# Local attention of a gated transformer: the last 128 queries' scores in other PSUM banks, ahead of the transposed probabilities of the 128 before them

## Chip, cores and metric

One core of one Trainium2 chip runs the whole kernel. The metric is the device time of one execution in microseconds (us). The kernel before was run three times.

## What is computed

The kernel is four blocks in a row on a stream x of 2048 tokens of width 256: cross-attention with 16 heads, a feed-forward block, a second cross-attention, and a small local transformer of two layers. Only the last one is touched. One of its layers, cut from the reference:

```python
h = shift_token(x)                       # the second half of the width moves one token on
q, k, v = split(h @ wqkv)                # 8 heads of 64
q, k = rotary_xpos(l2norm(q) * qs, l2norm(k) * ksc)
# windows of 128 queries; each looks at its own 128 keys and the 128 in front
sim = where(mask, -max, einsum('bhwid,bhwjd->bhwij', 8 * bq, bk))
o = einsum('bhwij,bhwjd->bhwid', softmax(sim), bv)
x = x + o @ wo
h = shift_token(x)
h = (h - mean(h)) / sqrt(var(h) + 1e-5) * lg + lb
a, g = split(h @ w1 + b1)
x = x + (a * gelu(g)) @ w2 + b2
```

## The kernel before

`windowed_attention` does the attention half of a layer, `shifted_ffn` the other half. Each is one block of the program: its instructions start only when all engines have ended the block in front. Every engine has an order written out by hand: a Python loop `for w in range(ST + 1)` with ST = 16 windows of 128 queries, in which each engine calls small functions for window w and its neighbours. Semaphores tie the engines together; `after(engine, name, n)` waits until n steps of that name are done. `base` is the count of windows in earlier layers. LAST or window 15 is the last, window 14 the one in front of it.

For one window, in the order of the data:

- TensorE `turn` transposes the rotated queries and keys (8 transposes, `d_rotated`) into PSUM banks 3 and 4. ScalarE `move` copies them to `qT` and `kT` (two copies). `qT` has one buffer.
- TensorE `score` makes the scores of 8 heads in two groups of 4 (g = 0, 1), into banks 3, 4 and 5, 6. VectorE `mask` adds the mask and `maxima` takes the row maxima, per group. ScalarE `expo` makes the exponentials of a group, with their sums.
- TensorE `turn_probs` transposes the probabilities of a group (8 transposes of `d_probs`), again into banks 3, 4 and 5, 6. ScalarE `move_probs` copies them to `d_probsT`.
- VectorE `invert` takes the inverse sums, GpSimd `expand` spreads them over the width, TensorE `spread` transposes them into bank 7, ScalarE `move_spread` copies them to `d_spread_in`.
- TensorE `apply` multiplies probabilities and values into bank 2 (`V_BANK`), VectorE `normalize` scales the result into `d_heads_outT`, TensorE `mix` multiplies by wo, again into bank 2, and VectorE `add` adds that to the stream `d_Z`.

While a window is in work, the projections of window w + 3 (split fp16 matmuls, lines 77 to 79) and the rotation of w + 2 run too. In the last windows there are none left. There the first 512 tokens of the feed-forward half are prepared instead, by class `ShiftedNorm`: `shift_half` (PSUM banks 0, 1 and later 6) and `move_shifted`, VectorE `statistics`, ScalarE `root` (a Sqrt of 128x4, which needs another activation table than Exp), VectorE `stage` (`d_shifted` normalised), TensorE `turn_h` (8 transposes into banks 0 and 1), ScalarE `move_h` (`d_hT`), and VectorE `split_h` (an fp16 pair `d_hT_hi`, `d_hT_lo`), which the first matmuls of `shifted_ffn` need.

The line that couples the two windows in TensorE's order is the wait in `turn_probs` (line 2196 of before):

```python
if g == 0:
    after(pe, "moved", base + min(w + 2, ST))
```

Banks 3 and 4 hold the turned queries and keys of window w + 1 until `move(w + 1)` has copied them, so the probabilities of window w can't be transposed before that; and `score(w + 1)` (line 2124) waits for `probs_moved`, so that it comes behind the transposed probabilities of window w.

## Time and profile before

| | before |
|---|---|
| median of 3 runs | 3123.19 us (3122.47 to 3125.54) |
| the profiled execution, its own time | 3124.35 us |
| its span in the profile | 3122.6 us |
| mean granted TensorE clock | 0.978 |
| layer 0: from `turn` of window 15 to the first feed-forward matmul | 2612.02 to 2646.91 us |
| layer 1: the same | 2980.19 to 3015.49 us |

The span runs from the first to the last instruction of the profiled execution; 1.75 us of the execution's own time lie around it. A row of the timeline names the start, the length, engine, line, operation, what is written and read, how many instructions were merged, and in brackets how long the engine sat idle before and who released it.

### The profile page before, as it was taken

Reading aid. Unit: us, or ns where it says so; the run is one execution under the profiler, and the core shown is the slowest. Engines: PE = TensorE matmul, PEld = TensorE weight load, DVE = VectorE, ACT = ScalarE, POOL = GpSimd, SP = SyncE. Lnnn points to the kernel's source line nnn. Section 1 sums busy time; section 2 is a strip of 40 time slices with the busy share of each in tenths; the row PEclk is TensorE's granted clock in tenths of the full one; section 3 lists DMA queues with packets and bytes.
Section 4 is the critical chain, followed back from the end, with each engine's and each line's share of the span. In section 5 each row is a group of like instructions: output and inputs, shape, how many; then the busy total and the mean of one; then the engine's idle time right before and its main releaser. Section 6 shows DMA issues by size and latency. Waiting matters only on the chain. (4 is left out here: it accounts for less than half of the span.)

```text
span 3122.6 us, 71606 instructions
## 1 busy us (share of the span) xinstructions
PE 2913.0 (93%) x29570; PEld 1454.7 (47%) x29570; DVE 2233.9 (72%) x2810; ACT 1944.9 (62%) x2644; POOL 518.9 (17%) x573
## 2 busy tenths in 40 slices
PE   5999999999999999999999899999996997989979
PEld 3444444444444444444444455222224766556755
DVE  6888888888889888888878875100006886768866
ACT  5665655656656656656556524899993775247642
POOL 0000000000001000000000010200002773247710
PEclk8999999999999999999999989999998999999999
DMA  2000000000000000000000011111101000000000
GB/s 81 9 2 7 3 2 7 3 2 9 2 7 4 2 7 3 2 2 3 2 2 2 28 38 63 56 28 36 29 19 53 15 8 25 36 14 18 5 1 28
DMA packets 30102, 51.69 MB, mean 17 GB/s; under 512 B 6136, under 2 KB 22603, under 8 KB 28619
## 3 DMA queue, kind: packets, MB, share of 16 engines
q1 hardware_dynamic: 29770, 46.91, 4.8%
q8 instruction: 253, 4.15, 0.6%
q14 instruction: 79, 0.64, 0.1%
HBM read 41.04 MB, written 5.83 MB: 15 GB/s over the span
## 5 line engine op out<-in xcount | busy, mean ns | idle before, releaser
L771 ACT ACTIVATE a_probs<-PS 128x1024 f32<-128x1024 f32 x928 | 950.0, 1025 | 572.2 <-PE PS L524 561.4
L537 PE MATMUL PS<-a_probs,a_V 64*64 64x512 f32 x7424 | 984.2, 590 | 6.7 <-DVE a_heads_outT L958 5.0
L1018 DVE TENSOR_TENSOR a_prob_sums<-a_prob_sums,a_probs 128x1024 f32<-128x1024 f32 x512 | 628.5, 1228 | 111.6 <-ACT a_probs L771 85.9
L1015 DVE SCALAR_TENSOR_TENSOR a_prob_sums<-a_probs,a_valid,a_prob_sums 128x1024 f32<-128x1024 f32 x384 | 508.6, 1325 | 73.1 <-ACT a_probs L771 59.4
L524 PE MATMUL PS<-a_Q_hi,a_K_hi 64*64 64x512 f16 x3712 | 390.4, 381 | 6.0 <-ACT a_probs L771 4.9
L524 PE MATMUL PS<-a_Q_hi,a_K_lo 64*64 64x512 f16 x3712 | 387.1, 377 | 2.2 <-issue 2.2
L524 PE MATMUL PS<-a_Q_lo,a_K_hi 64*64 64x512 f16 x3712 | 386.9, 377 | 0.0
L537 PEld LDWEIGHTS PS<-a_probs,a_V 64*64 64x64 f32 x7424 | 293.4, 133 | 168.1 <-issue 23.0
L1969 ACT ACTIVATE c_cT<-PS 128x1024 f32<-128x1024 f32 (+1 forms) x312 | 303.3, 1082 | 1.6 <-PE PS L1908 0.8
L67 POOL CAST a_heads_hi<-a_heads_outT 128x512 f16<-128x512 f32 x31 | 49.6, 1601 | 1444.8 <-DVE a_heads_outT L974 1444.8
L524 PEld LDWEIGHTS PS<-a_Q_hi,a_K_hi 64*64 64x64 f16 x3712 | 119.8, 106 | 260.3 <-issue 254.2
L524 PEld LDWEIGHTS PS<-a_Q_hi,a_K_lo 64*64 64x64 f16 x3712 | 120.6, 107 | 226.2 <-issue 222.0
L1987 DVE COPY c_outT<-PS 128x512 f32<-128x512 f32 x16 | 11.1, 692 | 296.4 <-PE PS L1908 296.4
L1908 PE MATMUL PS<-c_cT,c_Vh 128*32 128x512 f32 (+1 forms) x1248 | 221.1, 607 | 0.3 <-ACT c_wqkv L1969 0.3
L2275 ACT ACTIVATE d_probs<-d_scores,d_minus_max 128x256 f32<-128x256 f32 x256 | 127.0, 497 | 120.3 <-DVE d_minus_max L2440 120.3
L1888 PE MATMUL PS<-c_Qop,c_Kop 64*128 64x512 f16 (+1 forms) x832 | 154.6, 388 | 28.6 <-ACT c_cT L1969 6.7
L524 PEld LDWEIGHTS PS<-a_Q_lo,a_K_hi 64*64 64x64 f16 x3712 | 121.0, 107 | 88.7 <-issue 1.2
L1888 PEld LDWEIGHTS PS<-c_Qop,c_Kop 64*128 64x128 f16 (+1 forms) x832 | 38.6, 94 | 243.9 <-ACT c_cT L1969 194.5
L1969 ACT ACTIVATE c_wqkv<-PS 128x1024 f32<-128x1024 f32 (+1 forms) x104 | 112.9, 1085 | 0.0
L1908 PE MATMUL PS<-c_wqkv,c_Vh 128*32 128x512 f32 (+1 forms) x416 | 109.4, 605 | 0.0
L2543 POOL TENSOR_TENSOR d_crossed<-d_unit,d_tables 128x256 f32<-128x256 f32 x128 | 104.0, 842 | 6.1 <-DVE d_unit L2409 6.1
L2201 PE MATMUL PS<-ident,d_probs 128*128 128x128 f32 x512 | 69.0, 293 | 29.7 <-ACT d_kT L2290 29.7
(356 smaller groups left out, 4616.9 us busy)
## 6 DMA issues: line engine op xcount, KB each, us to landing
c_Qop<-q_part SPq DMA_DIRECT2D x96, 64.0 KB, 2.2
c_Kop<-k_part SPq DMA_DIRECT2D x96, 50.0 KB, 2.0
d_raw<-in_l1f_w_dram SPq DMA_DIRECT2D x18, 256.0 KB, 3.2
d_tables<-in_rotary_dram SPq DMA_DIRECT2D x2, 2048.0 KB, 11.4
X<-in_x_dram SPq DMA_DIRECT2D x2, 1024.0 KB, 9.4
out_dram<-X SPq DMA_DIRECT2D x8, 256.0 KB, 2.2
c_cT<-in_ctxT_dram SPq DMA_DIRECT2D x1, 1601.0 KB, 6.4
a_probs<-in_ctx_dram SPq DMA_DIRECT2D x3, 512.0 KB, 4.9
```

The lines of the kernel that those rows point to most:

```text
L67: return engine.tensor_copy(hi, x)
L524: last = nc.tensor.matmul(m.PS[64 * g:64 * g + 64, 2 * (n % 2) + h, :], k[rows, half_keys], q[rows, queries], start=(j == 0), stop=(j == l ...
L537: last = nc.tensor.matmul(m.PS[64 * h:64 * h + 64, PVB + g, :], V[e][rows, s, 64 * h:64 * h + 64], probs[n % 4][rows, h * BANK:(h + 1) * B ...
L771: nc.scalar.activation(probs[n % 4][:], m.PS[:, b0:b0 + 2, :].rearrange("p b c -> p (b c)"), ACT.Exp).then_inc(exped, 1)
L1015: nc.vector.scalar_tensor_tensor(out=sums, in0=new, scalar=valid[:, s:s + 1], in1=sums, op0=ALU.mult, op1=ALU.add).then_inc(summed, 1)
L1018: nc.vector.tensor_tensor(sums, sums, new, ALU.add).then_inc(summed, 1)
L1888: last = nc.tensor.matmul(m.PS[0:r, STEP_BANKS[n] + b, :], Kop[e][rows, c0:c0 + r], Qop[e][rows, q0:q0 + BANK], start=True, stop=True)
L1908: last = nc.tensor.matmul(m.PS[32 * q:32 * q + 32, 4 + e, :], Vh[e][0:r, t % CT, :], probs[2 * (t % 2) + q // 2][0:r, (q % 2) * BANK:(q % ...
L1969: nc.scalar.activation(probs[2 * (t % 2) + hp][0:r, :], m.PS[0:r, STEP_BANKS[n]:STEP_BANKS[n] + 2, :].rearrange("p b c -> p (b c)"), ACT.E ...
L2201: last = nc.tensor.transpose(m.PS[:, SCORE_BANK + 2 * g + p // 2, at:at + P], probs[:, 4 * g + p, kt * P:(kt + 1) * P], m.ident[:])
L2275: last = nc.scalar.activation(probs[:, p, :], scores[:, p, :], ACT.Exp, bias=minus_max[:, p:p + 1], accum_out=sums[:, p:p + 1])
L2543: last = nc.gpsimd.tensor_tensor(crossed[:, qk, :, a, :], unit[w % 2][:, qk, :, 1 - a, :], tables[:, 1, w, qk, a * 32:a * 32 + 32].unsquee ...
```

## The change

Only windows 14 and 15 of each layer's attention are touched, and the orders that four functions of the engines follow there.

- `score(15)` puts its first group into banks 0 and 1 (free after the projections and the shifted halves), its second into 5 and 6. It no longer waits for the copies of window 14's transposed probabilities, but for window 14's masks and for `shift_moved`. On TensorE it now stands ahead of `turn_probs(14)`.
- `turn_probs(14, 1)` goes to banks 3 and 4 as `turn_probs(14, 0)` does, and so waits until that one was copied. `turn_probs(15, 0)` waits for the copy of `turn_probs(14, 1)`.
- `mix(14)` and `turn_h` go behind `turn_probs(15)`.
- ScalarE: `move(15)` goes between the two halves of `expo(14)`; `expo(15, 0)` between the two `move_probs(14)`; `expo(15, 1)` behind `move_spread(14)`; `root` behind that, ahead of `move_probs(15)`, with no load of the Exp table after it.
- VectorE: `mask` and `maxima` of window 15 go into window 14's turn, around `invert(14)`; `add(14)` behind `stage`; `split_h` ahead of `add(15)`.

GpSimd's and SyncE's orders are as they were. No arithmetic is added or taken away.

```diff
--- before.py
+++ after.py
@@ -2106,6 +2106,9 @@
         inside = lambda w: 0 <= w < ST
 
         qk_bank = lambda w: SCORE_BANK + 2 if w == 1 else QK_BANK
+        LAST = ST - 1
+        score_bank = lambda w, g: QK_BANK if (w, g) == (LAST, 0) else SCORE_BANK + 2 * g
+        probs_bank = lambda w, g: SCORE_BANK if (w, g) == (LAST - 1, 1) else SCORE_BANK + 2 * g
 
         def after(engine, sem, count):
             if count > 0:
@@ -2121,14 +2124,18 @@
                 def score(w):
 
                     after(pe, "moved", base + w + 1)
-                    after(pe, "probs_moved", 2 * (base + w))
+                    if w == LAST:
+                        after(pe, "masked", 2 * (base + w))
+                        pe.wait_ge(s["shift_moved"], l * CH + 2)
+                    else:
+                        after(pe, "probs_moved", 2 * (base + w))
                     if w == 0:
                         after(pe, "kept", base + 2)
                     last_slot, slot = (w - 1) % K_RING, w % K_RING
                     for c in range(4):
                         for e in range(2):
                             rows = slice(64 * e, 64 * e + 64)
-                            bank, at = SCORE_BANK + c // 2 * 2 + e, c % 2 * 2 * P
+                            bank, at = score_bank(w, c // 2) + e, c % 2 * 2 * P
                             if last_slot < slot:
                                 last = nc.tensor.matmul(m.PS[:, bank, at:at + 2 * P], qT[rows, c, :],
                                                         kT[rows, c, last_slot:slot + 1, :].rearrange("p o n -> p (o n)"),
@@ -2195,10 +2202,14 @@
                     after(pe, "exped", 2 * (base + w) + g + 1)
                     if g == 0:
                         after(pe, "moved", base + min(w + 2, ST))
+                    if (w, g) == (LAST - 1, 1):
+                        after(pe, "probs_moved", 2 * (base + w) + 1)
+                    if (w, g) == (LAST, 0):
+                        after(pe, "probs_moved", 2 * (base + w))
                     for p in range(4):
                         for kt in range(2):
                             at = (p % 2 * 2 + kt) * P
-                            last = nc.tensor.transpose(m.PS[:, SCORE_BANK + 2 * g + p // 2, at:at + P],
+                            last = nc.tensor.transpose(m.PS[:, probs_bank(w, g) + p // 2, at:at + P],
                                                        probs[:, 4 * g + p, kt * P:(kt + 1) * P], m.ident[:])
                     last.then_inc(s["probs_turned"], 1)
 
@@ -2238,21 +2249,21 @@
                 turn(0)
                 project_v(2)
                 for w in range(ST + 1):
-                    if inside(w):
+                    if inside(w) and w < LAST:
                         score(w)
                     if inside(w + 3):
                         project_qk(w + 3)
-                    if inside(w - 1):
+                    if inside(w - 1) and w < LAST or w == ST:
                         if w == 1:
                             pe.wait_ge(s["rest_in"], 32 * (l + 1))
                         mix(w - 1)
                     if w == ST - 3:
                         tn.shift_half(pe, l, 0)
                         tn.shift_half(pe, l, 1)
-                    if w == ST - 1:
-                        tn.turn_h(pe, l, 0)
                     if inside(w + 1):
                         turn(w + 1)
+                    if w + 1 == LAST:
+                        score(LAST)
                     if inside(w + 3):
                         project_v(w + 3)
                     if inside(w + 4):
@@ -2260,6 +2271,9 @@
                     if inside(w):
                         for g in range(2):
                             turn_probs(w, g)
+                        if w == LAST:
+                            mix(w - 1)
+                            tn.turn_h(pe, l, 0)
                         spread(w)
                         apply(w, 0)
                         apply(w, 1)
@@ -2332,7 +2346,7 @@
 
                     after(act, "probs_turned", 2 * (base + w) + g + 1)
                     nc.scalar.activation(probsT[g][:].rearrange("p h k n -> p (h k n)"),
-                                         m.PS[:, SCORE_BANK + 2 * g:SCORE_BANK + 2 * g + 2, :].rearrange("p b n -> p (b n)"),
+                                         m.PS[:, probs_bank(w, g):probs_bank(w, g) + 2, :].rearrange("p b n -> p (b n)"),
                                          ACT.Copy).then_inc(s["probs_moved"], 1)
 
                 nc.scalar.preload_act_table(ACT.Sqrt)
@@ -2356,10 +2370,15 @@
                 nc.scalar.preload_act_table(ACT.Exp)
                 keep(2)
                 for w in range(ST + 1):
+                    if inside(w) and w < LAST:
+                        expo(w, 0)
+                    if w + 1 == LAST:
+                        move(LAST)
                     if inside(w):
-                        expo(w, 0)
                         expo(w, 1)
-                    if inside(w + 1):
+                    if w == LAST:
+                        tn.root(act, l, 0)
+                    if inside(w + 1) and w + 1 < LAST:
                         move(w + 1)
                     if inside(w + 3):
                         square(w + 3)
@@ -2367,6 +2386,8 @@
                         move_input(w + 4)
                     if inside(w):
                         move_probs(w, 0)
+                    if w + 1 == LAST:
+                        expo(LAST, 0)
                     if inside(w + 3):
                         value(w + 3)
                     if inside(w):
@@ -2377,9 +2398,6 @@
                     if w == ST - 3:
                         tn.move_shifted(act, l, 0)
                         tn.move_shifted(act, l, 1)
-                    if w == ST - 2:
-                        tn.root(act, l, 0)
-                        nc.scalar.preload_act_table(ACT.Exp)
                     if w == ST - 1:
                         tn.move_h(act, l, 0)
 
@@ -2431,7 +2449,7 @@
                     kind = 1 if w else 0
                     nc.vector.tensor_tensor(
                         scores[:, 4 * g:4 * g + 4, :],
-                        m.PS[:, SCORE_BANK + 2 * g:SCORE_BANK + 2 * g + 2, :].rearrange("p b (e n) -> p (b e) n", e=2),
+                        m.PS[:, score_bank(w, g):score_bank(w, g) + 2, :].rearrange("p b (e n) -> p (b e) n", e=2),
                         masks[:, kind:kind + 1, :].to_broadcast([P, 4, 2 * P]), ALU.add).then_inc(s["masked"], 1)
 
                 def maxima(w, g):
@@ -2500,18 +2518,24 @@
                 for w in range(ST + 1):
                     if inside(w - 1):
                         normalize(w - 1)
-                    if inside(w):
+                    if inside(w) and w < LAST:
                         if w == 0:
                             dve.wait_ge(s["rest_in"], 32 * (l + 1))
                         for g in range(2):
                             mask(w, g)
                             maxima(w, g)
-                    if inside(w - 1):
+                    if inside(w - 1) and w < LAST:
                         add(w - 1)
+                    if w + 1 == LAST:
+                        mask(LAST, 0)
+                        maxima(LAST, 0)
                     if inside(w + 2):
                         make_unit(w + 2)
                     if inside(w):
                         invert(w)
+                    if w + 1 == LAST:
+                        mask(LAST, 1)
+                        maxima(LAST, 1)
                     if inside(w + 2):
                         straighten(w + 2)
                     if inside(w + 3):
@@ -2524,8 +2548,10 @@
                         tn.statistics(dve, l, 0)
                     if w == ST - 1:
                         tn.stage(dve, l, 0)
+                        add(w - 1)
                         tn.statistics(dve, l, 1)
                 tn.split_h(dve, l, 0)
+                add(LAST)
 
             @block.gpsimd
             def _(pool):
```

TensorE, from `turn` of window 15 to the end of layer 0's attention, before. `d_rotated` is `turn`, `d_probs` `turn_probs`, `d_kT,d_qT` `score`, `d_expanded` `spread`, `d_probsT,d_V` `apply`, `d_wo` `mix`, `d_shifted` `turn_h`:

```order
L2173 MATMUL PS<-ident,d_rotated 128x128 x8
L2201 MATMUL PS<-ident,d_probs 128x128 x16
L2224 MATMUL PS<-ident,d_expanded 128x128 x4
L2214 MATMUL PS<-d_probsT,d_V 64x128 x16
L2133 MATMUL PS<-d_kT,d_qT 128x256 x8
L2189 MATMUL PS<-d_wo,d_heads_outT 128x256 x4
L2662 MATMUL PS<-ident,d_shifted 128x128 x8
L2201 MATMUL PS<-ident,d_probs 128x128 x16
L2224 MATMUL PS<-ident,d_expanded 128x128 x4
L2214 MATMUL PS<-d_probsT,d_V 64x128 x16
L2189 MATMUL PS<-d_wo,d_heads_outT 128x256 x4
```

The same place, changed:

```order
L2180 MATMUL PS<-ident,d_rotated 128x128 x8
L2140 MATMUL PS<-d_kT,d_qT 128x256 x8
L2212 MATMUL PS<-ident,d_probs 128x128 x16
L2235 MATMUL PS<-ident,d_expanded 128x128 x4
L2225 MATMUL PS<-d_probsT,d_V 64x128 x16
L2212 MATMUL PS<-ident,d_probs 128x128 x16
L2196 MATMUL PS<-d_wo,d_heads_outT 128x256 x4
L2688 MATMUL PS<-ident,d_shifted 128x128 x8
L2235 MATMUL PS<-ident,d_expanded 128x128 x4
L2225 MATMUL PS<-d_probsT,d_V 64x128 x16
L2196 MATMUL PS<-d_wo,d_heads_outT 128x256 x4
```

The scores of window 15 moved from behind window 14's `apply` to ahead of its `turn_probs`; `mix` of window 14 and `turn_h` moved behind window 15's `turn_probs`.

ScalarE, from window 14's exponentials to the end of the block, before:

```order
L2275 ACTIVATE d_probs,d_sums<-d_scores,d_minus_max 128x256 x8
L2289 ACTIVATE d_qT<-PS 128x512
L2290 ACTIVATE d_kT<-PS 128x4x128
L2334 ACTIVATE d_probsT<-PS 128x1024 x2
L2283 ACTIVATE d_spread_in<-PS 128x512
L2676 ACT_TABLE_LOAD
L2676 ACTIVATE d_work<-d_work 128x4
L2382 ACT_TABLE_LOAD
L2275 ACTIVATE d_probs,d_sums<-d_scores,d_minus_max 128x256 x8
L2334 ACTIVATE d_probsT<-PS 128x1024 x2
L2283 ACTIVATE d_spread_in<-PS 128x512
L2684 ACTIVATE d_hT<-PS,d_aff 128x512 x2
```

The same place, changed:

```order
L2289 ACTIVATE d_probs,d_sums<-d_scores,d_minus_max 128x256 x4
L2303 ACTIVATE d_qT<-PS 128x512
L2304 ACTIVATE d_kT<-PS 128x4x128
L2289 ACTIVATE d_probs,d_sums<-d_scores,d_minus_max 128x256 x4
L2348 ACTIVATE d_probsT<-PS 128x1024
L2289 ACTIVATE d_probs,d_sums<-d_scores,d_minus_max 128x256 x4
L2348 ACTIVATE d_probsT<-PS 128x1024
L2297 ACTIVATE d_spread_in<-PS 128x512
L2289 ACTIVATE d_probs,d_sums<-d_scores,d_minus_max 128x256 x4
L2702 ACT_TABLE_LOAD
L2702 ACTIVATE d_work<-d_work 128x4
L2348 ACTIVATE d_probsT<-PS 128x1024 x2
```

The copies `d_qT`, `d_kT` moved up by four exponentials, window 15's exponentials moved in between window 14's copies, and one of the two table loads is gone; the first table load of the feed-forward block (line 2676, Sqrt again) is gone too, since that table is still loaded.

## Rows read from the trace of the kernel before

**Rows 1.** The page: busy time of TensorE over the whole span.

```profile
PE 2913.0 (93%) x29570; PEld 1454.7 (47%) x29570; DVE 2233.9 (72%) x2810; ACT 1944.9 (62%) x2644; POOL 518.9 (17%) x573
```

**Rows 2.** Timeline of TensorE, end of layer 0's attention: start us, us, work [idle before].

```profile
2604.05 1.94 PE L2201 MATMUL PS<-ident,d_probs 128*128 128x128 f32 x16 [1.27 <-ACT d_kT L2290]
...
2612.02 1.04 PE L2173 MATMUL PS<-ident,d_rotated 128*128 128x128 f32 x8
2617.80 3.38 PE L2201 MATMUL PS<-ident,d_probs 128*128 128x128 f32 x16 [4.75 <-ACT d_kT L2290]
...
2621.77 1.97 PE L2214 MATMUL PS<-d_probsT,d_V 128*64 128x128 f32 x32
2623.67 2.00 PE L2133 MATMUL PS<-d_kT,d_qT 64*128 64x256 f32 x16
...
2633.76 1.97 PE L2662 MATMUL PS<-ident,d_shifted 128*128 128x128 f32 x8 [6.17 <-DVE d_shifted L2719]
...
2638.77 0.60 PE L2224 MATMUL PS<-ident,d_expanded 128*128 128x128 f32 x4
...
2642.12 1.99 PE L2189 MATMUL PS<-d_wo,d_heads_outT 128*128 128x256 f32 x8 [0.85 <-DVE d_heads_outT L2424]
2646.91 0.38 PE L77 MATMUL PS<-d_hT_hi,d_w_lo 128*128 128x512 f16 x1 [2.79 <-PEq L2114]
```

**Rows 3.** Timeline of ScalarE, the same stretch and columns.

```profile
2612.24 0.51 ACT L2275 ACTIVATE d_probs<-d_scores,d_minus_max 128x256 f32<-128x256 f32 x1 [3.68 <-DVE d_minus_max L2440]
...
2614.62 0.51 ACT L2275 ACTIVATE d_probs<-d_scores,d_minus_max 128x256 f32<-128x256 f32 x1 [0.31 <-DVE d_minus_max L2440]
...
2616.60 0.57 ACT L2289 ACTIVATE d_qT<-PS 128x512 f32<-128x512 f32 x1
2617.08 0.58 ACT L2290 ACTIVATE d_kT<-PS 128x512 f32<-128x512 f32 x1
2619.51 1.02 ACT L2334 ACTIVATE d_probsT<-PS 128x1024 f32<-128x1024 f32 x1 [1.85 <-PE PS L2201]
...
2622.14 0.59 ACT L2283 ACTIVATE d_spread_in<-PS 128x512 f32<-128x512 f32 x1
2622.75 1.28 ACT L2676 ACT_TABLE_LOAD   x1
2624.04 0.20 ACT L2676 ACTIVATE d_work<-d_work 128x4 f32<-128x4 f32 x1
...
2627.36 0.51 ACT L2275 ACTIVATE d_probs<-d_scores,d_minus_max 128x256 f32<-128x256 f32 x1 [1.82 <-DVE d_minus_max L2440]
...
2640.37 1.45 ACT L2684 ACTIVATE d_hT<-PS,d_aff 128x512 f32<-128x512 f32 x2
```

**Rows 4.** Timeline of VectorE, the same stretch and columns.

```profile
2623.84 0.69 DVE L2424 TENSOR_TENSOR d_heads_outT<-PS,d_spread_in 128x512 f32<-128x512 f32 x1 [4.73 <-PE PS L2214]
2624.85 1.22 DVE L2432 TENSOR_TENSOR d_scores<-PS,d_masks 128x1024 f32<-128x1024 f32 x1 [0.32 <-PE PS L2133]
...
2632.14 1.57 DVE L2719 TENSOR_SCALAR d_shifted<-d_shifted,d_mean,d_rstd 128x256 f32<-128x256 f32 x4
...
2644.15 0.42 DVE L2457 TENSOR_TENSOR d_Z<-d_Z,PS 128x256 f32<-128x256 f32 x1 [2.09 <-PE PS L2189]
...
2645.21 1.23 DVE L71 TENSOR_TENSOR d_hT_lo<-d_hT,d_hT_hi 128x1024 f16<-128x1024 f32 x1
```

**Rows 5.** Timeline of TensorE, end of layer 1's attention.

```profile
2980.19 1.04 PE L2173 MATMUL PS<-ident,d_rotated 128*128 128x128 f32 x8
...
3015.49 0.38 PE L77 MATMUL PS<-d_hT_hi,d_w_lo 128*128 128x512 f16 x1 [2.79 <-PEq L2114]
```

**Rows 6.** Timeline of TensorE, the first 128 queries of layer 0.

```profile
2419.20 2.78 PE L2201 MATMUL PS<-ident,d_probs 128*128 128x128 f32 x16 [2.26 <-ACT d_kT L2290]
```

**Rows 7.** Stretches: engines' busy us (instructions), PEclk the granted clock (1.00 is full).

```profile
2420.00:2423.00 3.00, 3.00 (x17) 2.67 (x17) 1.38 (x2) 2.79 (x6) 3.00 (x5) 0.52 0.00 0
...
2636.00:2638.00 2.00, 2.00 (x11) 2.00 (x10) 0.00 (x0) 0.52 (x1) 0.00 (x0) 0.50 0.00 0
```

## Prediction

> **What bounds the kernel now.** I read the page first: TensorE is busy for 2913.0 of 3122.6 us [rows 1], so time is to be had only where it waits or runs at a low clock. Then TensorE's timeline at the end of each attention block, since the change touches nothing else. From `turn` of window 15 to the first feed-forward matmul layer 0 takes 34.89 us and layer 1 takes 35.30 [rows 2, 5]. In layer 0 the reader should see four holes in brackets [rows 2]: 4.75 us before window 14's `turn_probs` (the copy to `d_kT` is late), 6.17 before `turn_h`, 0.85 before `mix(15)` and 2.79 at the block's end. The 6.17 is a masked wait: TensorE stands for `d_shifted`, VectorE makes that only after window 15's maxima and `invert`, and so after ScalarE's exponentials, which start at 2627.36 [rows 3]. So the tail is one dependent chain through three engines, and a window's work has nothing beside it.
>
> The holes cost twice. Sixteen `d_probs` transposes take 1.94 us at 2604.05 and 3.38 after the first hole; the eight of `turn_h` take 1.97 where `turn` needs 1.04 [rows 2]. In 2636 to 2638 the granted clock is 0.50, the lower level of 1.2 GHz [rows 7].
>
> **The change, step by step,** on layer 0's clock. Up to the end of `turn(15)` at 2613.06 nothing differs.
>
> 1. `move(15)` ahead of half of `expo(14)`. A group of four exponentials takes 1.98 us (2614.62 to 2616.60 [rows 3]). The first group starts at 2612.24, so the two copies, 1.06 us from 2616.60 to the end of `d_kT` [rows 3], now run from 2614.22 to 2615.28. TensorE followed that copy by 0.14 (2617.66 to 2617.80 [rows 2, 3]), so `score(15)` starts at 2615.4. The hole of 4.75 shrinks to 2.4. The second group of exponentials, 2615.2 to 2617.2, hides under `score(15)`, which takes 2.00 [rows 2].
> 2. `turn_probs(14, 0)` starts at 2617.4. Half of 1.94 is 0.97, so its copy, 1.02 long [rows 3], runs from 2618.5 to 2619.5. Here is the **new wait**: `turn_probs(14, 1)` uses the same banks and starts only at 2619.65, a hole of 1.3 us. Queued behind it are `spread(14)` and `apply(14)`, and everything later. It ends at 2620.6, `spread` and the first half of `apply` at 2622.1.
> 3. Meanwhile VectorE masks window 15: in before the mask starts 1.18 after `score` and the exponentials 2.51 after the mask [rows 2, 3, 4]. That gives 2619.1; ScalarE is free at 2619.45. Its four exponentials end at 2621.4, and only then does it copy `turn_probs(14, 1)`, to 2622.4. The second half of `apply(14)` starts 0.14 later, `turn_probs(15, 0)` at 2623.5, covered as far as ScalarE goes.
> 4. `move_spread(14)` costs ScalarE 0.4 (0.59 long, overlapping its neighbours [rows 3]); `expo(15, 1)` runs 2622.8 to 2624.8, `turn_probs(15, 1)` 2624.95 to 2625.9, `mix(14)` to 2627.8.
> 5. `root`: table load 1.29 from start to start and Sqrt 0.20 [rows 3], to 2626.3. Reciprocal some 0.2 (an estimate after the Sqrt of the same 128x4) and `stage` 1.57 [rows 4] give 2628.1 for `turn_h`. TensorE has just become free, so `mix(14)` is hidden by 0.3 us of slack; if it is later, `turn_h` is late by the rest. `move_probs(15)` runs beside this and is done before `apply(15)` needs it.
> 6. `turn_h` and `spread(15)`, 1.04 and 0.60 [rows 2] less overlap: `apply(15)` at 2629.6. `normalize` follows it by 2.07 (2621.77 to 2623.84 [rows 2, 4]) and takes 0.69, so `mix(15)` starts at 2632.45. `add(14)` (0.42) and `statistics` stand ahead of `normalize` on VectorE with 3.6 us for both, which I take to be enough; what they overrun would delay the end.
> 7. In before the end was `mix(15)` at 2642.12, `add`, both halves of `split_h`, first feed-forward matmul at 2646.91: 4.79 us. Now `split_h` (`d_hT` is ready: 1.45 of ScalarE [rows 3] after `spread`, some 2631.7) runs under `mix(15)`. What is left is 2.03 to the start of `add` (2642.12 to 2644.15), 0.42 for it, 0.47 from VectorE's last end to the matmul (2646.44 to 2646.91 [rows 2, 4]): 2.92. The first matmul falls at 2635.4.
>
> Saved: 2646.91 - 2635.4 = **11.5 us** in layer 0. Layer 1 took 0.4 more for the same work, so 35.30 - 23.4 = **11.9**. Sum **23.4 us**. The two table loads that vanish per layer give nothing here: one stood in ScalarE's idle time ahead of 2627.36, the other ahead of the first Gelu, for which TensorE, two tiles ahead in its order, doesn't wait. Behind the tail all work starts earlier by the same amount, the weight loads and output transfers too, since they are issued in the feed-forward block.
>
> **The unknown: the clock.** After a hole of 2.26 us the clock fell in the first window as well: 16 transposes took 2.78 instead of 1.94 [rows 6], and 2420 to 2423 ran at 0.52 with TensorE busy throughout [rows 7]. The new tail has holes of 2.4 and 1.3, nearest to that row. Ends: nothing lost, or one such stretch per layer, 3 us at half rate, 1.5 lost. I take the middle, 0.75 a layer, because ScalarE and not TensorE sets the pace in about half of the tail. Net: 23.4 - 1.5 = **21.9 us**. Against the profiled execution's own 3124.35 that is 3102.45; the median of the runs lies 1.16 lower, so **3101.3 us**.
>
> **A rule weighed: the table load.** The load takes 1.28 us, and the Sqrt starts 0.01 after it; the copy in front ended at 2622.73 and the load began at 2622.75 [rows 3]: no draining shows. The Trainium skill (ScalarE: Activation LUTs, What ACT_TABLE_LOAD costs) states some 1.38 us of drain beside 1.28 for each switch. By that rule step 5 would be 1.4 later a layer and the time 3104.1; the trace speaks against it.
>
> **Rivals.**
>
> - *Longer stretches at the low clock.* Before, `turn_h` and `turn_probs(15)` together lost 0.93 + some 1.5 us at 0.50 after a 6.17 hole [rows 2, 7]. That stretch of 5 us (2633.76 to 2638.77 [rows 2]) cost 2.4; with a shorter one of 1.5 beside it 3.9. The middle, 3.2 a layer, leaves 23.4 - 6.4 = 17.0 saved, 3106.2 us. For it: the tail and the first window shown both have low stretches. Against: the holes are less than half as long. Chance 0.27, the drain in the table load included.
> - *The exchange is worth nothing.* Banks 3 and 4 serialise copy, transpose and copy; if ScalarE's exponentials of window 15 hold up window 14's copies by more than step 3 has it, only step 7 and the shorter first hole remain, 1.9 + 0.6 a layer: 5 us, 3118.2. It needs 9 us of new waits a layer; I find 1.3 + 0.45. Chance 0.05.
> - *Slower.* The work is thinned so that the clock stays low from `score(15)` to `mix(15)`. That is 2.00 + 1.94 + 0.60 + 1.97 + 1.94 + 1.99 + 1.04 + 0.60 + 1.97 + 1.99 = 16.0 us of TensorE's work [rows 2]; at half rate it adds 16, less 1.0 of slack in steps 3 to 5: 15.0 against 11.5 saved, 3.5 a layer lost, 3130.2 us. It decides from 11.5 us of that work at the low level. Against: before, with nothing but transposes from 2633.76 on, `spread` at 2638.77 is back to 0.60 for four [rows 2], which is full rate. Chance 0.03. The Trainium skill (TensorE: Matmul & The Clock Gate, Part 4: PE-mode transpose) states that transposes don't count as busy for the clock; that would favour this case, and the row at 2638.77 contradicts it.
> - *More.* No low stretch, and the shorter ScalarE start of the feed-forward block lets VectorE run ahead: 25.5 saved, 3097.7. Chance 0.08.
> - That the change doesn't do what it says is excluded by the orders above: every step stands where it is described.
>
> **How the numbers follow.** The forecast has 0.57, its own range is 3099.8 (23.4 saved) to 3103. The range of 8 in 10 reaches into the longer low stretches and a little into "more": 3098.5 to 3107. About 0.2% or 6.2 us is what a measurement of this kernel can tell from no change. Faster by more than that: all but the last two failures, 0.93. Within it: "worth nothing" 0.04. Slower: 0.03.
>
> **What would show it.** Right: a hole of about 2.4 us between `turn(15)` and `score(15)`, one of 1.3 before the second half of `turn_probs(14)`, under 0.6 before `turn_h`, `split_h` under `mix(15)`, and 23.4 to 24.2 us from `turn(15)` to the first feed-forward matmul in both layers. Wrong: a hole over 3 us before `turn_probs(15)` or `turn_h` (ScalarE's chain was longer), the first matmul not following `add(15)`, `turn_probs` groups at over 3 us in both windows (the clock), or TensorE waits in the feed-forward block that weren't there before.

## The result, and the profile after

The changed kernel takes 3103.14 us (median of 6 runs, 3098.66 to 3105.24) against 3123.18 (6 runs, 3121.02 to 3125.54): 20.0 us less, ratio 0.9934 with a 95% interval of 0.9924 to 0.9945. The forecast was 3101.3 in a range of 3098.5 to 3107.

TensorE's timeline after, end of layer 0's attention, from `score(14)` to the first feed-forward matmul (start us, us, work, [idle before]). These are the rows that answer to [rows 2]:

```profile
2609.62 2.00 PE L2140 MATMUL PS<-d_kT,d_qT 64*128 64x256 f32 x16
...
2613.38 1.04 PE L2180 MATMUL PS<-ident,d_rotated 128*128 128x128 f32 x8
2616.67 3.60 PE L2140 MATMUL PS<-d_kT,d_qT 64*128 64x256 f32 x16 [2.26 <-ACT d_kT L2304]
2620.20 1.09 PE L2212 MATMUL PS<-ident,d_probs 128*128 128x128 f32 x8
2622.50 1.06 PE L2212 MATMUL PS<-ident,d_probs 128*128 128x128 f32 x8 [1.21 <-ACT d_probsT L2348]
...
2625.37 1.09 PE L2225 MATMUL PS<-d_probsT,d_V 128*64 128x128 f32 x16 [0.34 <-ACT d_probsT L2348]
2626.39 1.09 PE L2212 MATMUL PS<-ident,d_probs 128*128 128x128 f32 x8
2627.72 1.09 PE L2212 MATMUL PS<-ident,d_probs 128*128 128x128 f32 x8 [0.24 <-ACT d_probs L2289]
2628.65 1.89 PE L2196 MATMUL PS<-d_wo,d_heads_outT 128*128 128x256 f32 x8
2630.87 1.09 PE L2688 MATMUL PS<-ident,d_shifted 128*128 128x128 f32 x8 [0.32 <-DVE d_shifted L2745]
...
2632.32 1.97 PE L2225 MATMUL PS<-d_probsT,d_V 128*64 128x128 f32 x32
2635.14 1.99 PE L2196 MATMUL PS<-d_wo,d_heads_outT 128*128 128x256 f32 x8 [0.85 <-DVE d_heads_outT L2442]
2638.07 0.38 PE L77 MATMUL PS<-d_hT_hi,d_w_lo 128*128 128x512 f16 x1 [0.93 <-PEq L2117]
```

I call the stretch from the start of `score(14)` to the first feed-forward matmul the tail: 38.65 us in layer 0 before (2608.26 to 2646.91), 28.45 now. A hole is a time in which TensorE sits idle between two of its instructions. The hole of 4.75 is one of 2.26, the 6.17 before `turn_h` is 0.32, the 2.79 at the end 0.93. New are 1.21 before the second group of `turn_probs(14)`, 0.34 before the second half of `apply(14)` and 0.24 before the second group of `turn_probs(15)`. One row is out of line: `score(15)` at 2616.67 takes 3.60 us, where `score(14)` takes 2.00.

ScalarE and VectorE in the same tail, which answer to [rows 3, 4]:

```profile
2627.69 1.28 ACT L2702 ACT_TABLE_LOAD   x1
2628.98 0.20 ACT L2702 ACTIVATE d_work<-d_work 128x4 f32<-128x4 f32 x1
2629.09 1.92 ACT L2348 ACTIVATE d_probsT<-PS 128x1024 f32<-128x1024 f32 x2
...
2632.93 1.44 ACT L2710 ACTIVATE d_hT<-PS,d_aff 128x512 f32<-128x512 f32 x2
```

```profile
2629.43 1.38 DVE L2745 TENSOR_SCALAR d_shifted<-d_shifted,d_mean,d_rstd 128x256 f32<-128x256 f32 x4
...
2635.72 1.23 DVE L71 TENSOR_TENSOR d_hT_lo<-d_hT,d_hT_hi 128x1024 f16<-128x1024 f32 x1
2637.17 0.42 DVE L2475 TENSOR_TENSOR d_Z<-d_Z,PS 128x256 f32<-128x256 f32 x1 [0.23 <-PE PS L2196]
```

ScalarE goes from the table load to `move_probs(15)` without a pause. VectorE ends the split at 2636.95 and waits 0.23 for `mix(15)`: the split is hidden under it.

The granted clock (last columns: PEclk, DMA share, GB/s) over `score(15)`:

```profile
2616.00:2618.00 2.00, 1.33 (x6) 1.16 (x8) 0.26 (x1) 2.00 (x9) 0.00 (x0) 0.64 0.00 0
2618.00:2620.00 2.00, 2.00 (x12) 1.40 (x10) 1.20 (x1) 0.59 (x4) 0.00 (x0) 0.51 0.00 0
```

So nearly all of the 3.60 was spent at the lower level of 1.2 GHz. Shorter stretches place it closer: the granted clock is 1.00 up to 2616.5, so in layer 0 it fell at the end of the hole, 0.1 us before `score(15)` began, and it is back at 1.00 from 2620.0 on. That is 3.4 us at the lower level.

### The profile page after: what moved, and what is told of

Its sections match the earlier page's. It is cut to its first block and busy times, and to the rows that moved or that the text cites. A ratio compares the mean times of both kernels' runs of the same rounds, so it can differ in the third digit from the quotient of the medians.

```text
span 3103.5 us, 71604 instructions
## 1 busy us (share of the span) xinstructions
PE 2909.9 (94%) x29570; PEld 1454.0 (47%) x29570; DVE 2233.4 (72%) x2810; ACT 1937.6 (62%) x2640; POOL 518.1 (17%) x573
## 5 line engine op out<-in xcount | busy, mean ns | idle before, releaser
L2849 ACT ACTIVATE f_gelu<-PS,d_b 128x512 f32<-128x512 f32 x48 | 33.0, 687 | 86.3 <-PE PS L79 84.3
```

The lines of the kernel that those rows point to most:

```text
L2849: nc.scalar.activation(gelus[t % 2][:], m.PS[:, 2 * (t % 2) + 1, :], ACT.Gelu, bias=b1[:, 1, t:t + 1], scale=1 / FF_SCALE).then_inc(s["act ...
```

## Experiments

Two things differ from one execution of the same program to the next: where the clock falls, and how long the 2600 us ahead of the change take (`score(14)` of layer 0 starts between 2599.99 and 2609.62 in four profiles of the change). So I read each run by its tails, and by the sum from layer 0's `score(14)` to layer 1's first feed-forward matmul, which holds both tails and what lies between. Two columns say what the sum is made of: the time in which TensorE was idle, and the time at the lower clock. The second is worked out from the granted clock of stretches of 1 us (a stretch at 0.75 was at the lower level for half of its length). All in us, the last column apart from one profile of each:

| kernel | tail, layer 0 | between | tail, layer 1 | sum | idle in the sum | low clock in the sum | median (runs) |
| --- | --- | --- | --- | --- | --- | --- | --- |
| before | 38.65 | 329.52 | 39.06 | 407.23 | 56.7 | 34.1 | 3123.18 (6) |
| before, second | 38.61 | 330.82 | 38.08 | 407.51 | 56.5 | 34.1 | 3124.33 (1) |
| change | 28.45 | 329.78 | 28.54 | 386.77 | 40.0 | 17.1 | 3103.14 (6) |
| change, second | 26.87 | 332.73 | 26.87 | 386.47 | 40.1 | 17.1 | 3102.70 (5) |
| change, third | 26.85 | 332.47 | 26.87 | 386.19 | 39.7 | 17.1 | 3095.04 (1) |
| change, fourth | 28.52 | 328.99 | 28.49 | 386.00 | 41.4 | 13.6 | 3097.85 (1) |
| end undone | 28.73 | 330.84 | 28.76 | 388.33 | 43.6 | 13.6 | 3105.97 (4) |
| filler in the hole | 26.86 | 332.41 | 26.87 | 386.14 | 35.4 | 17.1 | 3102.35 (4) |
| Exp table back | 26.86 | 332.59 | 26.88 | 386.33 | 39.9 | 17.1 | 3103.10 (4) |
| late score | 34.75 | 329.74 | 35.37 | 399.86 | 47.3 | 34.1 | 3115.75 (7) |
| before, `move` split alone | 35.49 | 330.64 | 37.40 | 403.53 | 53.2 | 30.7 | 3120.58 (10) |
| `turn` first | 25.61 | 331.13 | 25.62 | 382.36 | 36.6 | 17.1 | 3099.36 (4) |
| `turn` first, second | 25.60 | 330.58 | 25.61 | 381.79 | 37.2 | 13.7 | 3098.22 (5) |

The change takes TensorE's idle time from 56.6 to 40.3 (means), 16.3 us less. The sum falls by 21.0, from 407.4 to 386.4, so the other 4.7 are the same work running faster: the time at the lower clock is 17 to 20 us shorter. The idle time of the filler's run leaves out the filler itself, which counts as work.

The end undone, the filler, `turn` first and `move` split alone shared a chip and the runs of before (3123.67). The change's second profile, the late score, the Exp table and `turn` first again shared another (3124.68), and the last three profiles a third (3120.97).

**The end undone.**

```diff
-                tn.split_h(dve, l, 0)
                 add(LAST)
+                tn.split_h(dve, l, 0)
```

> The change with its last part undone: VectorE adds window 15's mix before it splits d_hT, as before. I count the tail from the start of score(14) to the first feed-forward matmul: 38.65 us in layer 0 before, 28.45 with the change. Theory (the tail is a chain, and the split hides under mix(15)): the split's 1.9 us come back, tail 30.3 in both layers, 3.8 us more in all, about 3107. Rival (another engine holds the end of the block just as long, ScalarE's d_hT for one): tail within 0.3 of 28.45.

Measured: tail 28.73 and 28.76. The 30.3 had been set against 28.45, but here the clock did not fall and `score(15)` took 2.00; against the change's 26.87 at full clock the split costs 1.86 and 1.89, which is the theory's 1.9. By the number alone this is the rival's tail, within 0.3 of 28.45; what decides are the rows, `score(15)` at 2.00 and the hole at the end. TensorE's tail in this kernel:

```profile
2615.14 2.00 PE L2140 MATMUL PS<-d_kT,d_qT 64*128 64x256 f32 x16 [2.27 <-ACT d_kT L2304]
...
2636.80 0.38 PE L77 MATMUL PS<-d_hT_hi,d_w_lo 128*128 128x512 f16 x1 [2.79 <-PEq L2117]
```

The hole at the end is 2.79 again, where the change has 0.93. Of 3.8 us in the two tails only 2.0 arrive in the sum (388.33 against 386.4), since the stretch between was 330.84 here and not 332.6. That is the clock again: 13.6 us at the lower level here, 17.1 in the change's second and third profile.

**Filler in the hole.**

```diff
                     if w + 1 == LAST:
+                        pe.wait_ge(s["spread_moved"], base + w)
+                        for _ in range(10):
+                            nc.tensor.matmul(m.PS[:, OUT_BANK, :], zw_hi[0][:, 0, :], qkv[0][:, 0, 0:BANK],
+                                             start=True, stop=True)
                         score(LAST)
```

> The change with ten extra matmuls (fp16, 128x512, result never read, bank 7) in the hole ahead of score(15); the output is unaffected. Theory (score(15) takes 3.60 us instead of 2.00 because the clock fell in that hole): score(15) at 2.00, granted clock 1.00 through the tail, 1.3 to 1.6 us less per layer, tail 26.9 to 27.2, some 3 us less in all, 3100. Rival A (score(15) is slow for its banks or for ScalarE's reading beside it): it stays at 3.60 at a full clock, tail 28.4 or more. Rival B (the clock falls all the same, since it is not the hole alone): clock 0.5 over score(15), tail unchanged.

```profile
2613.52 2.32 PE L2268 MATMUL PS<-qkv_hi,d_zw_hi 128*128 128x512 f16 x10
2615.95 2.00 PE L2140 MATMUL PS<-d_kT,d_qT 64*128 64x256 f32 x16
...
2635.75 0.38 PE L77 MATMUL PS<-d_hT_hi,d_w_lo 128*128 128x512 f16 x1 [0.93 <-PEq L2117]
```

Measured: 2.00 and a tail of 26.86, as the theory has it; but the change itself, profiled again, does that too without filler. So the filler's effect is not shown, and its sum, 386.14, lies among the change's four, 386.00 to 386.77. The time, 3102.35, is not the 3100 expected. Rival A, that `score(15)` is slow for its banks or for ScalarE's reading beside it, is out by the change's own profiles: same banks, same neighbours, 2.00 at full clock.

**`turn` first.**

```diff
+                    if w + 1 == LAST:
+                        turn(LAST)
                     if inside(w - 1) and w < LAST or w == ST:
...
-                    if inside(w + 1):
+                    if inside(w + 1) and w + 1 < LAST:
                         turn(w + 1)
...
-                    if inside(w) and w < LAST:
-                        expo(w, 0)
                     if w + 1 == LAST:
                         move(LAST)
+                    if inside(w) and w < LAST:
+                        expo(w, 0)
```

> The change, with turn(15) ahead of mix(13) on TensorE and move(15) ahead of both halves of expo(14) on ScalarE. No work is added. Theory (chain: score(15) waits for d_kT, which waits for half of expo(14) only by ScalarE's order; mix(13) then fills part of the hole): the hole of 2.26 ahead of score(15) goes under 1.5, score(15) starts about 1.5 us earlier, and if the smaller hole keeps the clock, tail 25.6 to 26.0; if the clock falls all the same, 27.2. 5 us less in all at best, 3098. Rival (ScalarE is the chain, and putting two copies ahead of its exponentials delays them by 1.06 with nothing in return): tail 28.4 to 29.5.

```profile
2612.20 1.06 PE L2180 MATMUL PS<-ident,d_rotated 128*128 128x128 f32 x8 [0.84 <-DVE d_scores L2452]
2613.10 1.89 PE L2196 MATMUL PS<-d_wo,d_heads_outT 128*128 128x256 f32 x8
2614.92 2.00 PE L2140 MATMUL PS<-d_kT,d_qT 64*128 64x256 f32 x16
...
2619.36 1.06 PE L2212 MATMUL PS<-ident,d_probs 128*128 128x128 f32 x8 [1.41 <-ACT d_probsT L2350]
...
2634.98 0.38 PE L77 MATMUL PS<-d_hT_hi,d_w_lo 128*128 128x512 f16 x1 [0.93 <-PEq L2117]
```

Measured: `turn(15)` waits 0.84 for the mask of window 14's first group and `mix(13)` fills the rest, so `score(15)` starts 5.55 into the tail in place of 7.05. The copy wait ahead of `turn_probs(14)`'s second group grows from 1.21 to 1.41, and the tail is 25.6, within the theory. ScalarE had been idle ahead of its exponentials. Beside the change's second profile the first group of them starts later, 4.90 into the tail in place of 3.98, but the second starts at 6.87 in place of 6.92, and TensorE, which has `score(15)` to do first, waits for neither. Only the copy of `turn_probs(14)`'s first group now stands right behind the second exponentials, which is why that wait is longer.

**Before, with `move(15)` split off alone.**

```diff
                     if inside(w):
                         expo(w, 0)
+                    if w == ST - 2:
+                        move(w + 1)
+                    if inside(w):
                         expo(w, 1)
-                    if inside(w + 1):
+                    if inside(w + 1) and w != ST - 2:
                         move(w + 1)
```

> The kernel before, with one edit: move(15) between the two halves of expo(14) on ScalarE. Theory (that half of expo(14) was on the path): turn_probs(14) starts 2.2 to 2.4 us earlier, its second group waits for the second exponentials, tail 38.65 down to 36 to 36.5, 4 to 5 us less in all, 3118.5. Rival (the first hole is paid back later, because the scores of window 15 and all behind it hang on the copies of the probabilities): tail over 38, no change in time. What is left of the change's 10.2 a layer after this and the end's 1.9 belongs to the early score.

```profile
2616.21 1.06 PE L2201 MATMUL PS<-ident,d_probs 128*128 128x128 f32 x8 [2.36 <-ACT d_kT L2290]
2618.08 1.09 PE L2201 MATMUL PS<-ident,d_probs 128*128 128x128 f32 x8 [0.81 <-ACT d_probs L2275]
...
2631.71 1.97 PE L2665 MATMUL PS<-ident,d_shifted 128*128 128x128 f32 x8 [6.18 <-DVE d_shifted L2722]
```

Measured: `turn_probs(14)` starts 7.16 into the tail in place of 9.54, as expected, the second group waits 0.81 for its exponentials, and the tails are 35.49 and 37.40, one below and one above the 36 to 36.5 of the theory. Layer 1 kept less because the clock fell under the second group there (1.97 us for eight transposes against 1.09): its tail has 10.2 us at the lower level, layer 0's 6.8. The sum is 3.8 below the mean of before's two profiles, 407.4; the time is 0.9992 of before with an interval of 0.9982 to 1.0002, so the runs' times (3120.58 us where 3118.5 was expected) can't tell it from no change. The 6.18 before `turn_h` is untouched. The rival, tails over 38, is out.

**The change, again.**

> The change itself once more. In its first profile score(15) took 3.60 and 3.68 us at a low clock; in the run with the end undone, whose instructions are the same up to there, it took 2.00 behind the same hole of 2.27. Theory (whether the clock falls in that hole differs from one execution to the next): tail 26.8 to 27.0 where it doesn't fall, 28.4 to 28.5 where it does, nothing between but parts of the stretch; the runs spread over 3 us or more. Rival (the low stretch belongs to this program, and the end undone took it away): 28.45 in both layers again.

```profile
2615.74 2.00 PE L2140 MATMUL PS<-d_kT,d_qT 64*128 64x256 f32 x16 [2.28 <-ACT d_kT L2304]
...
2628.34 1.09 PE L2688 MATMUL PS<-ident,d_shifted 128*128 128x128 f32 x8 [0.32 <-DVE d_shifted L2745]
...
2635.54 0.38 PE L77 MATMUL PS<-d_hT_hi,d_w_lo 128*128 128x512 f16 x1 [0.93 <-PEq L2117]
```

Measured: full clock in both tails, 26.87. The five runs spread over 2.5 us, not 3 or more. The rival that the low stretch belongs to the program is out: the same program had 3.60 in one execution and 2.00 in the other. But the time did not fall by the 3.2 us that the two tails gained: 332.73 between against 329.78. One place between where it went is `turn_h` of the feed-forward block, which waits for `d_shifted` in every version (2.20 in before's first profile, 2.46 in the change's first, 2.59 in this one). This execution, `score(15)` first and then that place, in the columns of [rows 7]:

```profile
2616.00:2618.00 2.00, 2.00 (x19) 1.53 (x18) 1.08 (x1) 1.65 (x8) 0.00 (x0) 1.00 0.00 0
...
2667.00:2669.00 2.00, 0.00 (x0) 0.00 (x0) 1.62 (x10) 0.21 (x1) 0.00 (x0) 1.00 0.00 0
2669.00:2671.00 2.00, 1.54 (x8) 1.50 (x9) 1.97 (x5) 0.00 (x0) 0.00 (x0) 0.68 0.00 0
2671.00:2673.00 2.00, 2.00 (x7) 0.76 (x5) 1.03 (x2) 1.71 (x3) 0.00 (x0) 0.50 0.00 0
```

The change's first profile, at the same place:

```profile
2671.00:2673.00 2.00, 1.14 (x9) 1.02 (x10) 1.97 (x5) 0.01 (x1) 0.00 (x0) 1.00 0.00 0
```

In this execution the clock falls to 0.50 with TensorE busy, where the first profile had 1.00. Both have 17.1 us at the lower level in the sum: the first profile 3.4 in each tail and 10.2 between, this one none in the tails and all 17.1 between.

**Late score.** The early score alone undone; `move` inside `expo(14)`, the late `root` and `turn_h` and the end stay.

```diff
-                    if w + 1 == LAST:
-                        score(LAST)
...
                         apply(w, 0)
                         apply(w, 1)
+                    if w + 1 == LAST:
+                        score(LAST)
```

with `expo(15, 0)` moved in front of `expo(15, 1)` and both masks behind `invert(14)`.

> The change with the early score alone undone: score(15) behind apply(14), window 15's masks, maxima and exponentials behind it in one go; move(15) inside expo(14), turn_h behind turn_probs(15), root late and split_h under mix(15) all stay, and so do the banks. Theory (the early score overlaps two windows' chains and is the largest part): from score(15) at 12.5 to 13.2 into the tail, 1.18 + 2.51 + 4.1 of exponentials + 1.5 + 1.8 to turn_h and 7.2 to the end, tail 31 to 31.8 at a full clock against 26.9, so it is worth some 4.5 a layer, time some 3109. Rival (the order of turn_h and root and the end do the work, the early score only takes up time that ScalarE then makes TensorE wait for): tail under 28.5.

```profile
2616.95 1.94 PE L2212 MATMUL PS<-ident,d_probs 128*128 128x128 f32 x8 [1.81 <-ACT d_probsT L2348]
...
2621.80 2.00 PE L2140 MATMUL PS<-d_kT,d_qT 64*128 64x256 f32 x16
2627.62 1.97 PE L2212 MATMUL PS<-ident,d_probs 128*128 128x128 f32 x8 [3.83 <-ACT d_probs L2289]
...
2631.77 2.92 PE L2196 MATMUL PS<-d_wo,d_heads_outT 128*128 128x256 f32 x8
2634.53 1.04 PE L2687 MATMUL PS<-ident,d_shifted 128*128 128x128 f32 x8
```

Measured: tails 34.75 and 35.37, 3.0 and 3.6 us above the upper end of what I had expected. In layer 0 `score(15)` starts 14.88 in, not 13, behind the wait on shared banks (1.81) and transposes at the low clock. Then TensorE is idle for 3.83, the clock falls again (1.97 for eight transposes) and `mix(14)` takes 2.92 right ahead of `turn_h`. So putting the score late costs 7.9 and 8.5 us in the tails and 13.5 in the sum (3115.75 us against 3102.70 in time). Of the 7.9 and 8.5 idle time is 4.0 and 3.4, near the 4.5 expected; the rest is work at the lower clock, which lasts 34.1 us in the sum as in the kernel before. The early score itself is worth somewhat less than this: the late version keeps the shared banks, which only the early score needs, and waits 1.81 and 1.21 for them where `move` split alone, with banks of its own for the second group, waits 0.81. The rest of the change, without the early score, makes 407.4 into 399.9. The two single steps account for 3.8 (`move` split) and 2.0 (the end) of that; the order of `root` and `turn_h` was not undone alone.

**The Exp table back.**

```diff
                     if w == LAST:
                         tn.root(act, l, 0)
+                        nc.scalar.preload_act_table(ACT.Exp)
```

> The change with the load of the Exp table behind root put back, and so the second Sqrt load in the feed-forward block: two more loads of 1.28 us a layer. Theory (they lie beside other work): move_probs(15) ends 1.3 later but apply(15) starts 1.3 after its end, so tail within 0.3 of the change at the same clock, first Gelu 1.3 later, no new hole on TensorE, time within 2 us of 3103. Rival (ScalarE is the chain there): tail 1.3 longer, 2.6 us in all, or a new TensorE wait of up to 1.3 in the feed-forward block.

```profile
2623.75 1.28 ACT L2703 ACT_TABLE_LOAD   x1
2625.05 0.20 ACT L2703 ACTIVATE d_work<-d_work 128x4 f32<-128x4 f32 x1
2625.27 1.28 ACT L2381 ACT_TABLE_LOAD   x1
2626.56 1.94 ACT L2348 ACTIVATE d_probsT<-PS 128x1024 f32<-128x1024 f32 x2
...
2633.94 1.28 ACT L2703 ACT_TABLE_LOAD   x1 [3.51 <-PEq L2117]
...
2636.76 0.69 ACT L2850 ACTIVATE f_gelu<-PS,d_b 128x512 f32<-128x512 f32 x1
```

Measured: both loads are there (2625.27 and 2633.94), `move_probs(15)` starts 1.4 later in the tail and the first Gelu 1.1, tails 26.86 and 26.88 and a sum of 386.33: nothing that shows. ScalarE has room for it: in the change it is idle for 1.42 us behind `move_probs(15)`, here for none. So the two loads that the change drops are worth nothing by themselves.

**`turn` first, again.**

> The version with turn(15) ahead of mix(13) and move(15) ahead of expo(14), once more, for a closer time beside the change. Theory: tail 25.6 in both layers whatever the execution, since its holes are 0.84 and 1.41; time 2.5 to 5 us under the change. Rival (the gain of the first look was the clock's luck): a low stretch in at least one layer, time within 1 us of the change.

Measured: 25.60 and 25.61 once more, no low stretch in either tail. The mean of the two sums, 382.1, is 4.3 below the change's 386.4. In time, 3098.22 us (5 runs) beside 3102.70 for the change in the same rounds; ratio to before 0.9913, 0.9900 to 0.9927, against 0.9927, 0.9914 to 0.9941. The intervals overlap a little; the sums, 382.36 and 381.79 in two profiles against 386.00 to 386.77 in four, don't. It is the fastest version found. Of the 4.3 us the tails hold 2.5 where the change keeps its clock; the rest lies in the stretch between (330.6 to 331.1 against 332.6).

**Three more profiles, for the clock.**

> The change a third time, one look, for the clock. So far: low over score(15) in both layers (tail 28.45, 28.54) and then 329.8 us from layer 0's first feed-forward matmul to layer 1's score(14); or not low (26.87 twice) and then 332.7, with lower clock at the holes of the feed-forward block and the next block's start. Theory (each hole of about 2 us meets a fall of the clock in some executions, and the time of the whole moves with it): both tails either near 26.9 or near 28.5, from layer 0's score(14) to layer 1's 357 to 360 in all. Rival (the low stretch in the tail is rare, the first profile was an accident): 26.87 twice again.

> The same once more: same theories and numbers as for the third look.

> The kernel before, one more look, for the clock in its tails (38.65 and 39.06 in its profile, with about 4 us in each lost to the low clock). Theory (after a hole of 4.7 or 6.2 us the clock always falls, only the length of the low stretch differs): tails 38.4 to 39.4, turn_h at 1.97 in both layers. Rival (luck there too): a tail near 35 to 36 in one of the layers.

`score(15)` of layer 0 in the change's third profile, then in its fourth:

```profile
2607.04 2.00 PE L2140 MATMUL PS<-d_kT,d_qT 64*128 64x256 f32 x16 [2.26 <-ACT d_kT L2304]
```

```profile
2611.68 3.68 PE L2140 MATMUL PS<-d_kT,d_qT 64*128 64x256 f32 x16 [2.26 <-ACT d_kT L2304]
```

Measured: the change had 26.85 and 26.87 in its third profile, 28.52 and 28.49 in its fourth; from `score(14)` to `score(14)` 359.3 and 357.5, as expected. So two executions in four lose 1.6 us in each tail, always in both, and then pay less between: 329.8 and 329.0, against 332.7 and 332.5. The sums are 386.0 to 386.8 in all four. Two more versions with the same hole, the end undone and the Exp table back, did not lose it either, so it is two executions in six. Before has low stretches in both tails in both profiles, `turn_h` at 1.97 in all four tails; its second tail of layer 1 is 38.08, a little under the 38.4 expected. The time at the lower clock goes with this: 17.1 us in the sum in three profiles of the change, in the tails or out of them. The fourth has 13.6, and some 1.5 us more idle time. That what a tail keeps is lost between is what these profiles show; why is open.

## Why the prediction was right, and where it was off

The time, the sign and the mechanism were right. By its steps, with the tail at full clock (the change's second profile) beside it:

- *Step 1* put `score(15)` 7.14 into the tail behind a hole of 2.4. Measured 7.07 and 2.28. *Step 2*, the new wait of 1.3: 1.21. *Steps 3* and *4*, short waits only: 0.34 before the second half of `apply(14)`, 0.24 before the second group of `turn_probs(15)`.
- *Step 5*, `turn_h` at 2628.1, 19.84 into the tail: measured 19.67, with 0.32 of hole, so `mix(14)` is hidden, by as much as was stated. *Steps 6* and *7*: first matmul at 2635.4, 27.14 into it: measured 26.87. The split under `mix(15)` was put at 1.9 and is 1.86 and 1.89 by the run that undid it; the vanished table loads at nothing, and the run that put them back confirms it.
- Of the five signs that it named, one was met by no profile: 23.4 to 24.2 us from `turn(15)` to the first feed-forward matmul. It is 23.1 at full clock and 24.7 and 24.8 in the first profile. The range ran from no loss to the middle of the clock term, and a tail has either no loss or 1.6.
- So the two tails were to save 23.4 us at full clock, and save 24.0 (77.71 against 53.74; against before's second profile, whose layer 1 had less time at the lower clock, 23.0). Of the 24.0, 16.8 are holes (29.1 us in the two tails before, 12.3 after) and 7.2 are work that had run at the lower clock. The term that was too small is **the clock's 0.75 a layer, 1.5 us in all**. Where the low stretch falls on `score(15)` it costs 1.58 in layer 0 and 1.67 in layer 1, just over the upper end of the bound and not its middle: `score(15)` is wholly on the path, and ScalarE's share of the tail gives no cover there. Where it does not, 2.4 us are lost between the tails instead (332.6 against a mean of 330.2 before), which the sum had at nothing: it said that behind the tail all work only starts earlier. Either way 2.4 to 3.3 are paid, not 1.5, and the sum falls by 407.4 - 386.4 = 21.0 us where 21.9 was forecast. The median moved by 20.0; the last 1 us is within the spread of the runs. That the forecast came so close is in a small part luck: the holes gave a little more than it had, the clock took more.
- The table load at 2627.69 begins 0.03 after ScalarE's exponentials end and is followed by the Sqrt at 2628.98, 0.01 after its own end, in the changed kernel too. So the drain of 1.38 us that the Trainium skill (ScalarE: Activation LUTs, What ACT_TABLE_LOAD costs) adds to each switch shows in neither kernel.
- In the changed kernel's first profile the clock is back at full from 2620.0, while `score(15)`, which is no transpose, was running. The Trainium skill (TensorE: Matmul & The Clock Gate, Part 4: PE-mode transpose) says that transposes don't count as busy for the clock; the changed tail doesn't test that. The version with `move` split alone repeats the row that spoke against it: from 2631.71 on it runs nothing but transposes, at 0.50, and `spread` at 2636.41 is back to 0.60 for four.
- *Longer stretches at the low clock*, priced at 17.0 saved, did not happen: a tail has 3.4 us at the lower level or none. *The exchange is worth nothing* is refuted by the late score, which loses 7.9 and more a layer. *Slower* would have needed the low level over some 11.5 us of TensorE's work, counted at full clock; it was 1.6 a layer. *More* had two conditions. No low stretch in the tails did occur in two profiles, but the sum did not fall with it; and VectorE does not run ahead in the feed-forward block, where `turn_h` waits 2.46 to 2.59 in the change's four profiles, not less than 2.20.

## What to carry to other kernels

At the end of this pipelined loop the work of one item had nothing beside it, and each engine's written order became the critical path. In a loop like it, look there for a step that only waits because its banks or its place in a queue follow the steady state's rule. A second set of banks that has just come free lets two items' chains overlap; here that was worth more (some 7 us a layer) than any single step (1.3 to 3.2). Price a hole twice, as idle time and as the clock it may cost, and where the same executions have several holes of 2 us, judge by a stretch that holds them all.

## What the runs showed of the hardware that I had not expected

The same program had the granted clock fall behind the same 2.26 us hole in two executions of four, in both layers or in neither, though the tails are 360 us apart. What one hole kept, later holes lost: the tails differ by 3.2 us, the sums by 0.8 at most. Three of the four have 17.1 us at the lower clock in the sum, with 6.8 of it in the tails or none. And ten matmuls that kept TensorE busy through that hole brought nothing that the sum shows (386.14 against 386.0 to 386.8); its time at the lower clock is 17.1 us too.
